# Layer norms centred and scaled as blocks, log sums and router weights kept in PSUM banks, and spare identity products in TensorE's opening waits

## The reference, cut to what matters

```
x = x + attn_a(norm(x))   # token mixing, k, v, r projections, a scan with a fixed decay, norm, Wo
x = x + ffn(norm(x))      # 8 experts of 512, all of them computed, weighted per token
x = x + attn_b(norm(x))   # small MLPs for r, k, v and low rank gates, a scan whose state is 16 heads of 8x8, norm, MLP
x = x + ffn(norm(x))
```

```
norm(x)   = (x - mean(x)) / sqrt(var(x) + eps)
decay     = exp(-0.74 * sigmoid(tanh(...)))      # attn_b; the running product of it over tokens is exp of a running sum
router    = softmax(z @ w_router); gates = softmax(z @ w_gating / 0.1)
cw        = router * gates;  cw = cw / (sum(cw) + 1e-9)
ffn(z)    = sum over experts e of cw[e] * (silu(z @ w_gate[e]) * (z @ w_up[e])) @ w_down[e]
```

## Time and profile before

| | |
|---|---|
| median of three runs | 961.81 us |
| the profiled execution, its own time | 961.01 us |
| its span (first to last instruction) | 959.3 us |
| mean granted TensorE clock | 0.954 of 2.4 GHz |
| TensorE busy | 864.3 us, 90% of the span |
| VectorE busy | 589.2 us, 61% |
| ScalarE, GpSimd busy | 401.9 us (42%), 411.2 us (43%) |
| chain that ended last, by engine | TensorE 54%, VectorE 17%, issue 4%, ScalarE 2%, GpSimd 1% |
| largest group on TensorE | the down products, 304.2 us busy and 38.0 us idle before them |

### The profile page before, as it was taken

The page is one execution under the profiler, slowest core; times in us unless marked ns, Lnnn a source line. Parts: engine busy times, 40 slices in busy tenths (PEclk is TensorE's granted clock), DMA queues, the critical chain, the costliest instruction groups (busy, mean ns, idle before and its releaser), DMA issues.

```text
span 959.3 us, 13871 instructions
## 1 busy us (share of the span) xinstructions
PE 864.3 (90%) x5170; PEld 728.3 (76%) x5170; DVE 589.2 (61%) x979; ACT 401.9 (42%) x878; POOL 411.2 (43%) x296
## 2 busy tenths in 40 slices
PE   4399999989898899999987969798999789999997
PEld 1387987778767779997665658687998668788886
DVE  6559644388918993239589896988113968532322
ACT  5143347633264233335655346123333244453333
POOL 3434311056703876536244543567653534211111
PEclk9599999999899999999997789999999989999999
DMA  9300000011001100022111001111002211000000
GB/s 283 84 1 1 1 1 1 1 44 44 23 23 44 45 23 23 1 88 89 44 44 45 22 23 45 45 44 44 12 1 88 89 52 48 1 1 12 1 1 12
DMA packets 20711, 35.88 MB, mean 37 GB/s; under 512 B 3062, under 2 KB 9636, under 8 KB 20644
## 3 DMA queue, kind: packets, MB, share of 16 engines
q1 hardware_dynamic: 20644, 35.00, 11.1%
HBM read 21.36 MB, written 13.63 MB: 36 GB/s over the span
## 4 chain that ended last, share of the span: by engine, by line
PE 54%; DVE 17%; issue 4%; ACT 2%; POOL 1%; DVEq 0%; ACTq 0%; POOLq 0%
PE bank L1219 53%; DVE sh_buf L1661 1%; DVE normed L1548 1%; DVE states L1873 1%; DVE state L1777 1%; DVE low L1675 1%; DVE w_a L1875 1%; DVE state L1788 1%; DVE scr L1881 1%; DVE backs L1856 1%; DVE work L1752 1%; DVE work L1771 1%; PE bank L1233 0%; ACT sh_buf L1048 0%; DVE quad L1743 0%
## 5 line engine op out<-in xcount | busy, mean ns | idle before, releaser
L1661 DVE TENSOR_TENSOR sh_buf<-sh_buf,bank 128x512 f32<-128x512 f32 x256 | 172.6, 683 | 276.7 <-PE bank L1219 229.4
L1219 PEld LDWEIGHTS bank<-w_down,sh_buf 128*128 128x128 f32 x2048 | 283.9, 197 | 74.5 <-DVE sh_buf L1661 47.1
L1219 PE MATMUL bank<-w_down,sh_buf 128*128 128x128 f32 x2048 | 304.2, 285 | 38.0 <-DVE sh_buf L1661 37.9
L1048 ACT ACTIVATE sh_buf<-bank 128x512 f32<-128x512 f32 x256 | 152.8, 598 | 305.9 <-PE bank L1219 233.7
L1219 PE MATMUL bank<-z_lo,w_hi 128*128 128x512 f32 x512 | 238.9, 467 | 0.0
L1219 PE MATMUL bank<-z_hi,w_hi 128*128 128x512 f32 x512 | 205.5, 401 | 0.0
L1219 PE MATMUL bank<-z_hi,w_lo 128*128 128x512 f32 x512 | 205.0, 400 | 0.0
L945 POOL TENSOR_TENSOR x<-x,y_weighted 128x512 f32<-128x512 f32 x64 | 85.2, 1331 | 248.6 <-ACT y_weighted L1162 248.6
L1219 PEld LDWEIGHTS bank<-z_hi,w_hi 128*128 128x128 f32 x512 | 98.3, 192 | 24.1
L1219 PEld LDWEIGHTS bank<-z_lo,w_hi 128*128 128x128 f32 x512 | 100.0, 195 | 10.8 <-issue 4.1
L1219 PEld LDWEIGHTS bank<-z_hi,w_lo 128*128 128x128 f32 x512 | 100.0, 195 | 7.8 <-issue 0.7
(11 more groups left out here) (207 smaller groups left out, 992.9 us busy)
## 6 DMA issues: line engine op xcount, KB each, us to landing
trans_spill<-state SPq DMA_DIRECT2D x16, 512.0 KB, 2.6
backs<-trans_spill SPq DMA_DIRECT2D x16, 512.0 KB, 3.3
backs<-keep_spill SPq DMA_DIRECT2D x4, 1024.0 KB, 5.5
x<-in_x SPq DMA_DIRECT2D x4, 256.0 KB, 5.7
backs<-in_w_gate SPq DMA_DIRECT2D x4, 256.0 KB, 5.7
backs<-in_w_up SPq DMA_DIRECT2D x4, 256.0 KB, 5.9
keep_spill<-rkv SPq DMA_DIRECT2D x4, 256.0 KB, 2.5
keep_spill<-low SPq DMA_DIRECT2D x4, 256.0 KB, 2.6
```

What stands on the lines that cost most here:

```text
L1048: act.activation(s_buf[:, m % 2, :], bank_of("gate", m)[:], ACT.Silu).then_inc(S["silu_done"], 1)
L1219: return pe.matmul(dst, lhs, rhs, start=start, stop=stop, **kw)
L1661: dve.tensor_tensor(h_buf[:, m % 4, :], s_buf[:, m % 2, :], bank_of("up", m)[:], ALU.mult).then_inc(S["h_done"], 1)
```

## The change

Six edits, all at once:

1. A norm's four instructions become two blocks of 128x512 on VectorE: `centre` (x minus the mean, broadcast), which needs only the statistics and so may run while GpSimd makes one over the root, and `norm`, which multiplies by it. `centre` is a task of its own in the plan. The two signalling instructions of `mid` go.
2. `log` writes its running sums into a bank (`lend_log` takes one for it) in place of the SBUF tile, and `decay` reads them there.
3. The router's differences, exponentials and sums lie in the router's own bank, which so stays taken until `combine` is done; `combine` has eight instructions in place of nine, and one fused multiply-add in place of several.
4. The very last `weigh` and `add` (ScalarE, then GpSimd) become four fused instructions on VectorE (`add_last`).
5. `keep_busy` puts spare products of the identity with itself on TensorE, written to the bank that is taken next anyway: 18 ahead of the first `mid_T`, 12 ahead of the transposes of `mid` norm 0, 16 ahead of those of `ffn` norm 0.
6. The plan's durations follow, one weight changes, and the whole `LEAD` table has new numbers, so that the order of nearly everything behind the opening is another.

```diff
@@ -71,8 +71,8 @@
...
-WEIGHT = dict(pe=1.60, act=1.20, dve=1.31, pool=1.10, sp=1.02)
...
+WEIGHT = dict(pe=1.60, act=1.10, dve=1.31, pool=1.10, sp=1.02)
...
-def norm(kind, n, after, z_act, z_after=(), stats=1.72, norm=1.37, port=False):
+def norm(kind, n, after, z_act, z_after=(), stats=1.72, norm=0.7, port=False, centre=True):
     k = kind + "_"
     return [dve((k + "stats", n), stats, *after, *z_after, port=port),
             pool((k + "stats", n), 1.35, on("dve", k + "stats", n)),
-            dve((k + "norm", n), norm, on("pool", k + "stats", n)),
+            dve((k + "centre", n), 0.7, on("dve", k + "stats", n), port=centre),
+            dve((k + "norm", n), norm, on("pool", k + "stats", n), on("dve", k + "centre", n), port=True),
...
@@ -1036,9 +1043,9 @@
 
             def ffn_exp(q):
                 act.wait_ge(S["rl_used"], q + 1)
-                pr = probs[:].rearrange("p (g s) e -> p g s e", s=2)
-                act.activation(pr[:, :, 0, :], pr[:, :, 0, :], ACT.Exp).then_inc(S["probs_rdy"], 1)
-                act.activation(pr[:, :, 1, :], pr[:, :, 1, :], ACT.Exp, scale=10.0).then_inc(S["probs_rdy"], 1)
+                pr = route_part(q, 64, 2 * G, E).rearrange("p (g s) e -> p g s e", s=2)
+                act.activation(route_part(q, 128, G, E), pr[:, :, 0, :], ACT.Exp).then_inc(S["probs_rdy"], 1)
+                act.activation(chances_b[:], pr[:, :, 1, :], ACT.Exp, scale=10.0).then_inc(S["probs_rdy"], 1)
...
-                act.activation(cumdec[:, 1:G + 1, :], td, ACT.Exp, scale=-DECAY / 2).then_inc(S["ew_exp"], 1)
-                act.activation(invdec, td, ACT.Exp, scale=DECAY / 2).then_inc(S["ew_exp"], 1)
+                act.activation(cumdec[:, 1:G + 1, :], logs(j), ACT.Exp, scale=-DECAY / 2).then_inc(S["ew_exp"], 1)
+                act.activation(invdec, logs(j), ACT.Exp, scale=DECAY / 2).then_inc(S["ew_exp"], 1)
...
+            def keep_busy(bank, n):
+
+                for _ in range(n):
+                    mm(bank[:, 0:P], ident[:], ident[:])
+
             def ln_transposes(kind, j):
                 n = LN[kind, j]
                 name = BANK[kind + "_z", j]
+                take(name)
+                if j == 0 and kind in ("mid", "ffn"):
+                    keep_busy(bank_named[name], 12 if kind == "mid" else 16)
                 pe.wait_ge(S["ln_norm"], n + 1)
-                take(name)
...
                 name = BANK["mid_T", q]
+                take(name)
+                if q == 0:
+                    keep_busy(bank_named[name], 18)
                 pe.wait_ge(S["kvr_used"], B * (u + 1))
-                take(name)
...
-                free[name] = (S["rl_used"], q + 1)
+                free[name] = (S["cw_rdy"], q + 1)
...
+            def lend_log(j):
+
+                name = BANK["log", j]
+                lent_log[j] = free.get(name)
+                free[name] = (S["ew_exp"], 2 * (j + 1))
...
-            def ln_normalise(n, tiles, last_sem="ln_norm"):
+            def per_tile(v):
+                return v.unsqueeze(2).broadcast_to((P, G, C))
+
+            def ln_centre(n, tiles):
+                return dve.tensor_tensor(normed[:, n % 2], tiles, per_tile(mean_var[:, n % 2, :, 0]), ALU.subtract)
+
+            def ln_scale(n):
                 dve.wait_ge(S["ln_rstd"], n + 1)
-                for i in range(G):
-                    ins = dve.tensor_scalar(normed[:, n % 2, i, :], tiles[:, i, :], mean_var[:, n % 2, i, 0:1],
-                                            rstd[:, n % 2, i:i + 1], ALU.subtract, ALU.mult)
-                    if i < G - 1 or not last_sem:
-                        step.inc(ins)
-                if last_sem:
-                    ins.then_inc(S[last_sem], 1)
+                step.wait()
+                return dve.tensor_tensor(normed[:, n % 2], normed[:, n % 2], per_tile(rstd[:, n % 2, :]), ALU.mult)
...
-            def mid_norm(q):
-                ln_normalise(LN["mid", q], inner(q), None)
-                step.wait()
-
-                dve.tensor_scalar(tick[:, 0:1], neg_half[:], 1.0, None, ALU.mult).then_inc(S["inner_read"], 1)
-                dve.tensor_scalar(tick[:, 1:2], neg_half[:], 1.0, None, ALU.mult).then_inc(S["ln_norm"], 1)
...
-                dve.tensor_tensor(probs[:], lg, lmax[:].unsqueeze(2).broadcast_to((P, 2 * G, E)),
+                dve.tensor_tensor(route_part(q, 64, 2 * G, E), lg, lmax[:].unsqueeze(2).broadcast_to((P, 2 * G, E)),
                                   ALU.subtract).then_inc(S["rl_used"], 1)
...
-                pr = probs[:].rearrange("p (g s) e -> p g s e", s=2)
-                step.inc(dve.tensor_reduce(psum_[:], probs[:], AX_X, ALU.add))
-                step.inc(dve.tensor_tensor(w, pr[:, :, 0, :], pr[:, :, 1, :], ALU.mult))
-                step.wait()
-                step.inc(dve.reciprocal(prec[:], psum_[:]))
...
-                step.inc(dve.reciprocal(pscale[:], cwsum[:]))
-                step.wait()
-                dve.tensor_tensor(w, w, pscale[:].unsqueeze(2).broadcast_to((P, G, E)), ALU.mult).then_inc(S["cw_rdy"], 1)
+                chances_a, sums_a, total, inverse = route_part(q, 128, G, E), route_part(q, 192, G), route_part(q, 196, G), route_part(q, 200, G)
+                step.inc(dve.tensor_reduce(sums_a, chances_a, AX_X, ALU.add))
+                step.inc(dve.tensor_reduce(sums_b[:], chances_b[:], AX_X, ALU.add))
+                step.inc(dve.tensor_tensor(w, chances_a, chances_b[:], ALU.mult))
+                step.wait()
+                step.inc(dve.tensor_tensor(both[:], sums_a.rearrange("p n e -> p (n e)"), sums_b[:], ALU.mult))
+                step.inc(dve.tensor_reduce(total, w, AX_X, ALU.add))
+                step.wait()
+
+                step.inc(dve.scalar_tensor_tensor(out=total, in0=both[:].unsqueeze(2), scalar=1e-9, in1=total, op0=ALU.mult, op1=ALU.add))
+                step.wait()
+                step.inc(dve.reciprocal(inverse, total))
+                step.wait()
+                dve.tensor_tensor(w, w, inverse.broadcast_to((P, G, E)), ALU.mult).then_inc(S["cw_rdy"], 1)
...
+                if lent_log[j]:
+                    dve.wait_ge(*lent_log[j])
                 step.inc(dve.tensor_copy(cumdec[:, 0, :], cumdec[:, G, :]))
                 for i in range(G):
                     step.wait()
-                    step.inc(dve.scalar_tensor_tensor(out=td[:, i, :], in0=td[:, i, :], scalar=1.0,
-                                                      in1=td[:, i - 1, :] if i else log_end[:], op0=ALU.add, op1=ALU.add))
-                step.wait()
-                dve.tensor_copy(log_end[:], td[:, G - 1, :]).then_inc(S["ew_log"], 1)
+                    step.inc(dve.scalar_tensor_tensor(out=logs(j)[:, i, :], in0=td[:, i, :], scalar=1.0,
+                                                      in1=logs(j)[:, i - 1, :] if i else log_end[:], op0=ALU.add, op1=ALU.add))
+                step.wait()
+                dve.tensor_copy(log_end[:], logs(j)[:, G - 1, :]).then_inc(S["ew_log"], 1)
...
+                step.inc(ln_scale(n))
...
+            def add_last():
+
+                q, e = PASSES - 1, E - 1
+                dve.wait_ge(S["y_full"], PASSES * E)
+                dve.wait_ge(S["x_added"], PASSES * E - 1)
+                dve.wait_ge(S["cw_rdy"], PASSES)
+                for i in range(G):
+                    ins = dve.scalar_tensor_tensor(out=xt(BLOCKS - 1)[:, i, :], in0=bank_of("y", PASSES * E - 1)[:, i * P:(i + 1) * P],
+                                                   scalar=cw[:, q % 2, i, e:e + 1], in1=xt(BLOCKS - 1)[:, i, :], op0=ALU.mult, op1=ALU.add)
+                    if i < G - 1:
+                        step.inc(ins)
+                step.wait()
+                ins.then_inc(S["x_added"], 1)
...
+                elif task == "mid_centre":
+                    dve.wait_ge(S["ln_mv"], LN["mid", n[0]] + 1)
+                    ln_centre(LN["mid", n[0]], inner(n[0])).then_inc(S["inner_read"], 1)
+                    dve.wait_ge(S["inner_read"], n[0] + 1)
+                elif task == "back_centre":
+                    dve.wait_ge(S["ln_mv"], LN["back", n[0]] + 1)
+                    step.inc(ln_centre(LN["back", n[0]], scr2[:]))
...
+                elif task.endswith("_centre"):
+                    dve.wait_ge(S["ln_mv"], LN[kind, n[0]] + 1)
+                    step.inc(ln_centre(LN[kind, n[0]], xt(n[0] % BLOCKS)))
                 elif task.endswith("_norm"):
-                    ln_normalise(LN[kind, n[0]], xt(n[0] % BLOCKS))
+                    ln_scale(LN[kind, n[0]]).then_inc(S["ln_norm"], 1)
```

56 lines of the change are left out of this document (28 added, 28 removed).

## The result

The changed kernel takes 929.74 us (median of 4 runs, 928.23 to 932.41) against 961.96 for the one before: a ratio of 0.9671, 95% interval 0.9645 to 0.9697. The forecast was 951.8, with a range down to 940. The profiled execution of after has a span of 928.3 us, 31.0 less than before's 959.3.

A forecast was written before the change was run, and what follows sets the result against it. TensorE's work, its waits and its loss at the lower clock were taken to bound the kernel. From 961.0 us, opening 6.5, end 1.2 and middle 2.3 less gave 951.0, plus 0.8 for the median: 951.8, range 940 to 962.

The forecast's parts named there:

- the middle: Between opening and end: 8.8 us of removed waits and clock loss, less added waits of 2 and 4.5: 2.3 us less.
- The prediction's own sign of being wrong: Transposes of 1.1 us behind spare products, or TensorE's waits from 60 us to its last product outside 50 to 63 us.
- the wait of 2.12 us goes: Middle, `combine`: hardly a large SBUF operand is left, so TensorE's one wait of 2.12 us there disappears.
- The added waits: Middle: new waits of TensorE, 2 us more at the `log` and 4.5 us between slots 23 and 24.
- The table taken as 0: The new `LEAD` table, which moves all the rest of the order, was costed at 0.
- Norms: Middle: two blocks wait less than four instructions, 1.6 us at each of two places, 3.2; 3.5 more from the clock.
- The `log`: Middle: sums reading a bank would save 5.0 us, but the new order fills the place, so no gain.
- Opening: Up to the first slots: 3.1 us earlier, 1.1 of work done ahead, 2.3 from the clock: 6.5 us less.
- The first: Rival: all waits behind GpSimd go and no new ones come, 934 us; 13 in 100.
- The second: Rival: the norm blocks wait as long as the four instructions did, so 3.2 and 3.5 are not won, 958.5 us; 15 in 100.
- the third: Rival: the clock falls in the opening all the same, spare products cost 0.52 us each, 963.4 us; 7 in 100.
- VectorE's long pieces: Rival: VectorE's long pieces between two `hidden` tasks become the bound and stall TensorE, slower, 966 us with 75 of waits; 11 in 100.

The follow-up runs named there:

- three single edits: The changed kernel in its own order with one old operation put back at a time: norms 935.55 us, log sums 933.93 us, router's weights (`combine`) 945.82 us.
- all at once: The changed kernel in its own order with the old norms, log sums and router's weights all put back, new tail and spare products kept: 951.91 us.

## Why the prediction was wrong, by its steps

**The direction held, and so did it that small instructions of VectorE wait for GpSimd; the middle was mis-sized.** Forecast 2.3 us less, measured 26.2: of the span's 31.0, 1.4 is the end, and 3.4 the opening (at the eighth slot after is 66.95 - 64.69 = 2.26 us ahead and has 1.1 us of `mid_out` done). The prediction's own sign of being wrong came: TensorE's waits from 60 us on are 40.7 us, not within 50 to 63. By the table, 19.4 us of waits went from the eighth slot on, where the forecast had 1.2 more (5.3 removed, 6.5 added), and 8.1 us that the lower clock had cost, where it had 3.5.

**The step that failed first is that of `combine`:** "the wait of 2.12 us goes". It priced the one place where TensorE was seen to wait in before's order, and nothing for the clock behind it. In the new order the old `combine` costs 13.6 to 16.1 us, of which 8 are waits in the traces: three of its passes meet GpSimd there, where two did before, and TensorE waits behind two of them. The rows for more were there: 2.23 us for 32 columns said that each such instruction can wait for a whole one of GpSimd, wherever a new order puts it. So the new order and the operands in a bank make their gain together: neither the wait of 4.20 us nor its price could be seen in before's trace. How much of before's own time went to `combine` isn't shown; the new one was not run in before's order.

**The added waits failed next:** 6.5 us that did not come. Between slots 23 and 24 VectorE has its 13 us as forecast, but TensorE, which I gave 9 us of work, was busy nearly all through:

```profile
103.55:117.66 14.11, 13.99 (x80) 1.00 0.00 1
```

Gates of later slots, `w_a` products and the router filled it. At the last `log`, VectorE took 2.06 + 0.96 us for the four sums, where three alone took 6.00; TensorE has no wait over 0.4 us between 521 and 550 us, where I had 7.27 and 2 more. The order has a large part in that: with the new table alone no wait for `hidden` is over 4.4 us, and with the log in SBUF again in after's order none is over 4.2.

**The table taken as 0** was worth 8 us with before's operations.

**Norms:** 3.2 us at two places, and 3.5 of the clock. Measured 5.8 in after's order and 6.7 in before's, so the sum was near, but by luck: in before's order the two places gave 1.1 us of wait and the clock 0.4, and most came at the `log`'s wait. VectorE's time doesn't explain it in either order (47.1 us for the blocks against 46.8 in before's; 38.4 for the 48 blocks in after's, 35.5 for the 96 instructions put back). What the blocks save in after's order is the step behind GpSimd's part, since the first block runs ahead of it or beside it: 0.69 us in place of 1.36 to 1.6, or of 3.14 where the four meet GpSimd. By the traces 2.9 us of it are waits and 1.8 the clock.

**The `log`** costed at no gain: 4.2 us by the medians, but only 0.3 us of wait behind a `log` in the trace; what the clock makes of one wait is as much, and whether the `log` gave anything in this order stays open. The 26.1 us of three single edits against the 22.2 of all at once are within the same doubt; in waits the three come to 13.3 us in the traces, all at once to 10.6.

**Opening:** 6.5 forecast, 3.4 came. The chain lost its slow products as costed; the term that failed is the last, the slots at 1.2 GHz (2.3 us, came as 0.4) and the 1.2 us of the first slot, both behind the waits of 1.20 and 1.42 us, which I had taken as closed. One reason for the first is the price of a spare product: forecast 0.27 us, measured 0.23, so that 16 of them filled 3.74 us. They hid in full, and all together are worth 3.3 us. **End:** 1.2 forecast, 1.4 came.

**The rivals.** The first, all waits behind GpSimd gone and no new ones, at 934, was nearest; it had 13 in 100. It too counted only visible waits, so that it came near for other reasons than its own. The second, that the blocks wait as long as the four, held at the first of its two places in before's order (4.42 us against 4.23) and half at the other (3.33 against 4.18); in after's order the blocks take 0.78 and 0.86 us in the mean, and its 958.5 is far off. The clock did fall in the opening, only later and shorter than the third had it. VectorE's long pieces never bound.

## What to carry over

When small instructions of VectorE on SBUF tiles can meet GpSimd, look for them in the new order and not in the old trace: wherever GpSimd works beside them, each addition or multiplication with two SBUF operands, each `tensor_scalar` and each copy may wait for the rest of one of its instructions. With one operand in a bank none waited here. A table of numbers that orders a program is fitted to its tasks and their durations, and can be neither kept nor judged apart from them. Before a term is called right because its number came, look in the trace whether it came at its place. Differences below some 5 us on this kernel need the waits and the clock's stretches added up beside the times, since the clock took between 2 and 7 us behind one and the same wait.
